# The last block of the second and third feed-forward also prepares the next attention's first batch

## The chip, the cores and the metric

One core of a Trainium2 chip runs the whole program. The metric is the device time of one execution in microseconds, lower is better. The program is one launch that computes four layers, each an attention and a feed-forward network, on 8 batches of 256 tokens of 128 numbers, with 512 context tokens a batch.

## The reference, cut to what matters

All eight steps add to `x`, and each one normalises `x` over its last axis first:

```python
x = x + _L0_xattn_ref(_layernorm(x), ctx, ctx, ...)     # A0
x = x + _L0_ffn_ref(_layernorm(x), ...)                 # F0, quantised
x = x + _L1_xattn_ref(_layernorm(x), ctx, ...)          # A1
x = x + _L1_ffn_ref(_layernorm(x), ...)                 # F1, 8 experts + shared one
x = x + _L2_xattn_ref(_layernorm(x), ctx, ctx, ..., mask)  # A2
x = x + _L2_ffn_ref(_layernorm(x), ...)                 # AS (causal attention) and F2, 8 experts
x = x + _L3_xattn_ref(ctx, ctx, _layernorm(x), mask, ...)  # A3
x = x + _L3_ffn_ref(_layernorm(x), ...)                 # F3, 8 experts
```

An attention has 16 heads of 8 numbers. Its queries come from `x`, its keys and values from the context (in AS all three come from `x`):

```python
scores = jnp.einsum('bhqd,bhkd->bhqk', q, k) / scale    # plus a mask in A2 and A3
attn = jax.nn.softmax(scores, axis=-1)
ctx = jnp.einsum('bhqk,bhkd->bhqd', attn, v)
```

An expert layer computes gates for each token and adds up `comb[t, e] * (act(x @ w1[e] + b1[e]) @ w2[e] + b2[e])` over its experts.

## The kernel before

The kernel is written in nine phases (`PHASES`): A0, F0, A1, F1, A2, AS, F2, A3, F3. Each engine has its own instruction stream, written out in order by hand, and the streams meet at semaphores. For each phase and each kind of event the class `Counts` knows which count a semaphore has by then, so `wait(pe, "max_done", cnt.at(...) - BACK[i])` means: PE goes on when the maximum that last read this buffer is done.

**An attention phase** goes through 8 batches, and each batch through 4 groups of 4 heads. For each group PE makes *plain* scores (queries as rows, `scores`, L1036, 8 matmuls into the three PSUM banks `ps_s`), DVE takes the maximum of each row (`maximum`, L1435, or L1438 with A2's mask added), POOL splits the maxima into bf16 parts (`split_maxima`, L685 to L688), PE turns them (`maxima_T`, L1086 and L1088, into the bank `ps_m`), ACT copies them into `qmx` (L890), and only then PE makes the *transposed* scores with the maximum already taken off (`scores_T`, L1051, banks `ps_t`; in A2 a mask is put in first, `opening_mask`, L1062). ACT takes their exponential (L845), and PE multiplies with the values (`values`, L1078, bank `ps_av`). In the steady state the plain scores run two groups ahead.

Before a batch can start it needs its keys, queries and values. `misc` makes them on PE in `ps_m`: "K" (L1120, fp32, 128x512), "XT" (L1108, two transposes of the normalised tokens), "Q" (L1113, 128x256) and "V" (L1126, four of 128x128). ACT reads each of them out (L868, L859, L863, L875). POOL normalises the tokens (L700) and splits keys and queries into a high and a low part (`split_k`, L666 and L668; `split_q`, L674 and L676). The SP queue saves these to DRAM (`save`, L488) and loads them back as strips of heads (`load_strips`, L523 and L524, into `kst` and `qst`). `output_bias` (L1094, L1097; DVE L1423) makes a constant that is added to the result. `take_misc` makes PE wait for the last reader of `ps_m`.

**An expert phase** (F1, F2, F3) goes through 4 blocks of 512 tokens, and each block through its experts (9 in F1, 8 in F2 and F3). `first_product` (L1281) makes the hidden layer of expert `e + 1` in `ps_t` and `ps_s[2]` while ACT applies the activation to that of expert `e` (L985, or L983 in F2); `second_product` (L1303) multiplies it by the second weights into `ps_s[0]` or `ps_s[1]`, and DVE adds it up with its gate (`accumulate`, L1667 and L1669). After the last expert `result` adds to `x_tok` (L1691) and takes the statistics of the tokens (L1367 to L1379), and POOL makes the reciprocal deviation (`power`, L640). The split weights (`w_parts`, L970 and L785) lie in `kst[1]`, and the third pair of F1 in `kst[0]`; the split tokens `x_hi`, `x_lo` are `k_hi`, `k_lo`; `combT` is part of `kf`. Every one of these is also an attention's buffer.

Between an expert phase and the next attention all engines wait for the last block's result, although batch 0 needs only the tokens of block 0:

```python
            def attention(ph):
                if ph != "AS":
                    wait(pe, "acc_done", cnt.start("acc_done", ph))
                    wait(pe, "h_done", cnt.start("h_done", ph))
                    wait(pe, "x_new", cnt.start("x_new", ph))
```

After that come K, XT, Q, V, the biases, then 16 plain scores of groups 0 and 1 with `maxima_T` of group 0 after the thirteenth, and then the batches. POOL waits likewise before it normalises batch 0 (`rstd_done`), and DVE before its first maximum.

## Time and profile before

| | |
|---|---|
| runs | 1944.78, 1940.82, 1942.22 us, median 1942.22 |
| profiled execution | 1943.53 us, of which the span is 1941.7 us |
| PE busy | 1749.6 us (90%) |
| DVE, ACT, POOL busy | 1149.1 (59%), 1084.7 (56%), 589.3 us (30%) |
| F1's last matmul, A2's first exponential | 834.1, 863.1 us |
| F2's last matmul, A3's first exponential | 1455.7, 1487.7 us |

The times of a row count from the start of the span. PE is busy nearly all the time, so the places of interest are those where it is not: among them are the two stretches in the last rows of the table, 29 and 32 us, in which one phase has ended and the next has not got going. The chip grants TensorE one of two clocks, 1.2 or 2.4 GHz; "PEclk" is the mean of it as a share of 2.4 GHz.

### The profile page before, as it was taken

The numbers are of one execution on the slowest core, as the hardware profiler recorded it, in microseconds if no ns is written. First come the engines' busy times: TensorE is split into PE (matmuls) and PEld (weight loads), VectorE is DVE, ScalarE is ACT, GpSimd is POOL, SyncE is SP. The second block draws the span as 40 slices with busy tenths as digits, with TensorE's granted clock in tenths as the row PEclk, the third lists the DMA queues.
The fourth block names the chain that finished last, engine by engine and source line by source line (L and its number), as shares of the span: only waits on it lengthen the run. The fifth ranks groups of instructions, "written<-read, shape, count | busy, mean of one in ns | idle before, by whom it ended". The sixth has DMA issues, their size and how long they took to land.

```text
span 1941.7 us, 38864 instructions
## 1 busy us (share of the span) xinstructions
PE 1749.6 (90%) x14438; PEld 1188.5 (61%) x14476; DVE 1149.1 (59%) x3394; ACT 1084.7 (56%) x2172; POOL 589.3 (30%) x1171
## 2 busy tenths in 40 slices
PE   5999955899979999979999999979996999989997
PEld 2555524455548889944444455558883555569997
DVE  5788846688852332236777656636664888633443
ACT  1788831488864444426677755533332888844442
POOL 5344212233312221122333344323324344122221
PEclk9999977699999999969999999979995999989999
DMA  4443200455300000023323134300004454100000
GB/s 142 128 126 121 76 16 14 128 169 175 104 18 1 1 1 1 1 87 113 102 92 99 40 115 134 92 1 1 1 1 129 146 155 137 35 1 7 6 7 6
DMA packets 114854, 132.38 MB, mean 68 GB/s; under 512 B 14934, under 2 KB 78700, under 8 KB 114668
## 3 DMA queue, kind: packets, MB, share of 16 engines
q1 hardware_dynamic: 114668, 129.90, 22.1%
q8 instruction: 117, 1.92, 0.4%
q14 instruction: 69, 0.57, 0.1%
HBM read 83.45 MB, written 46.40 MB: 67 GB/s over the span
## 4 chain that ended last, share of the span: by engine, by line
PE 76%; issue 7%; DVE 7%; ACT 6%; POOL 1%; DMA 1%; SPq 0%; POOLq 0%; DVEq 0%
PE ps_s L1303 14%; PE ps_av L1078 13%; PE ps_s L1036 12%; PE ps_t L1281 9%; PE ps_t L1051 4%; PE ps_s L1281 3%; ACT prob L845 3%; PE ps_t L1062 3%; DVE mx L1435 3%; PE ps_m L1086 2%; PE ps_m L1134 2%; PE ps_m L1120 2%; PE ps_m L1126 2%; PE ps_m L1113 2%; PE ps_t L1064 1%
## 5 line engine op out<-in xcount | busy, mean ns | idle before, releaser
L845 ACT ACTIVATE prob<-ps_t 128x512 f32<-128x512 f32 (+1 forms) x1152 | 616.5, 586 | 169.8 <-PE ps_t L1051 161.7
L1435 DVE TENSOR_REDUCE mx<-ps_s 128x1 f32<-128x512 f32 x768 | 487.3, 683 | 110.9 <-PE ps_s L1036 109.4
L1036 PE MATMUL ps_s<-kst,qst 32*128 32x512 f32 (+2 forms) x1280 | 387.1, 490 | 43.3 <-DVE mx L1435 22.4
L1303 PEld LDWEIGHTS ps_s<-w_ffn,prob 128*128 128x128 f32 x2688 | 314.2, 192 | 8.3
L1303 PE MATMUL ps_s<-w_ffn,prob 128*128 128x128 f32 x2688 | 318.4, 276 | 0.0
L1036 PEld LDWEIGHTS ps_s<-kst,qst 32*128 32x128 f32 x1280 | 166.7, 192 | 241.4 <-issue 98.1
L1051 PE MATMUL ps_t<-qmx,kst 32*128 32x256 f32 (+1 forms) x2304 | 306.4, 334 | 6.1 <-ACT prob L845 6.1
L1078 PE MATMUL ps_av<-prob,vaug 128*32 128x256 f32 (+1 forms) x4608 | 307.2, 386 | 2.7 <-ACT avs L886 2.7
L985 ACT ACTIVATE prob<-ps_t,b1c 128x512 f32<-128x512 f32 x204 | 125.3, 685 | 240.9 <-PE ps_t L1281 240.9
L1669 DVE SCALAR_TENSOR_TENSOR avs<-ps_s,comb,avs 128x128 f32<-128x128 f32 x336 | 94.6, 344 | 260.4 <-PE ps_s L1303 260.4
L785 POOL TENSOR_TENSOR kst<-w_ffn,kst 128x512 fp32r<-128x512 f32 x100 | 127.1, 1273 | 371.3 <-ACT kst L970 371.3
L1438 DVE CUSTOM_DVE_ANT_0 junk<-ps_s,mask_q 128x512 bf16<-128x512 f32 x256 | 167.6, 687 | 67.6 <-PE ps_s L1036 66.0
L1051 PEld LDWEIGHTS ps_t<-qmx,kst 32*128 32x128 f32 x2304 | 188.5, 189 | 15.4 <-ACT prob L845 10.1
L685 POOL CAST mpart<-mx 128x8 bf16<-128x8 f32 x160 | 34.8, 217 | 517.3 <-DVE mx L1435 304.8
L1281 PE MATMUL ps_t<-k_hi,kst 128*128 128x512 f32 x600 | 184.8, 416 | 6.2 <-ACT xfT L947 2.4
L1078 PEld LDWEIGHTS ps_av<-prob,vaug 128*32 128x32 f32 x4608 | 122.3, 111 | 93.8 <-ACT avs L886 5.1
L1281 PEld LDWEIGHTS ps_t<-k_hi,kst 128*128 128x128 f32 x600 | 107.8, 193 | 27.6 <-DVE prob L1654 3.6
L1438 DVE CUSTOM_DVE_ANT_0 junk<-ps_s,caus_q 128x128 bf16<-128x128 f32 (+1 forms) x256 | 82.3, 354 | 70.9 <-PE ps_s L1036 69.1
L640 POOL TENSOR_TENSOR rstd<-veps,neg_half 128x2 f32<-128x2 f32 (+1 forms) x60 | 48.4, 807 | 246.2 <-DVE means L1379 246.2
L890 ACT ACTIVATE qmx<-ps_m 128x256 fp32r<-128x256 f32 x160 | 61.5, 385 | 109.5 <-PE ps_m L1088 109.3
L1062 PE MATMUL ps_t<-mask_T,ident_b 128*128 128x512 bf16 x218 | 76.8, 394 | 14.4 <-ACT prob L845 12.0
L1281 PE MATMUL ps_t<-k_lo,kst 128*128 128x512 f32 x300 | 86.1, 396 | 0.0
(209 smaller groups left out, 2151.3 us busy)
## 6 DMA issues: line engine op xcount, KB each, us to landing
kst<-k_parts SPq DMA_DIRECT2D x128, 256.0 KB, 3.4
qst<-q_parts SPq DMA_DIRECT2D x160, 128.0 KB, 3.6
k_parts<-k_hi SPq DMA_DIRECT2D x64, 256.0 KB, 3.0
q_parts<-q_hi SPq DMA_DIRECT2D x80, 128.0 KB, 2.4
ctxT<-in_ctxT SPq DMA_DIRECT2D x32, 256.0 KB, 2.7
k_parts<-k_lo SPq DMA_DIRECT2D x32, 256.0 KB, 3.5
q_parts<-q_lo SPq DMA_DIRECT2D x40, 128.0 KB, 2.4
w_ffn<-in_F_w SPq DMA_DIRECT2D x18, 256.0 KB, 3.3
```

Of the source, the lines that this page charges most:

```text
L785: pool.tensor_tensor(halves(wl), first_weights(ph, e), halves(wh.bitcast(F32)), ALU.subtract).then_inc(sig["wl_done"], 1)
L845: nc.scalar.activation(row[:, S * kt:S * kt + w], ps_t[TURN[unit(ph, g, n) % 8]][:, 0:w], ACT.Exp).then_inc(sig["exp_done"], 1)
L985: nc.scalar.activation(h[:, c, :], src, ACT.Gelu, bias=b1c[:, 4 * e + c:4 * e + c + 1]).then_inc(sig["h_done"], 1)
L1036: pe.matmul(dst, qst[p][strip, g, q * 128:(q + 1) * 128], kst[p][strip, g, 0:nk], start=True, stop=True).then_inc(sig["s_ready"], 1)
L1051: mm = pe.matmul(dst, kst[p][strip, g, kt * 128:(kt + 1) * 128], qmx[strip, g % 2, seen(ph, kt):], start=not opened, stop=not opened or c ...
L1062: pe.matmul(bank[:, :].rearrange("p (c s) -> p c s", c=2), ident_b[:, :], mask_T[:, 2 * kp:2 * kp + 2, :], start=True, stop=False)
L1078: mm = pe.matmul(ps_av[32 * j:32 * j + 32, q0:S], vaug[p][:, kt, HG * g + j, :], prob[:, buf, j, S * kt:S * (kt + 1) - q0], start=(kt == 0 ...
L1281: mm = pe.matmul(ps_h[c][:, :], w[:, 128 * c:128 * (c + 1)], x[:, :], start=(n == 0), stop=(n == 2))
L1303: mm = pe.matmul(dst, h[:, c, 128 * q:128 * (q + 1)], w2c, start=(c == 0 and not bias), stop=(c == nc_h - 1))
L1435: dve.tensor_reduce(mx[:, buf, i:i + 1], src, AX.X, ALU.max, negate=True).then_inc(sig["max_done"], 1)
L1438: dve.tensor_tensor_reduce(junk[:, TURN[i], 0:nk], src, m, -1.0, 3.0e38, ALU.add, ALU.min, mx[:, buf, i:i + 1])\
L1669: ins = dve.scalar_tensor_tensor(out=acc[:, q, :], in0=src, scalar=comb[:, q, n:n + 1], in1=acc[:, q, :], op0=ALU.mult, op1=ALU.add)
```

## The change

The last block of F1 and F2 also makes K, XT, Q and V of the next attention's batch 0, each behind one expert's second product, and its output bias (in F1 also that of AS) around the fifth expert. POOL normalises batch 0 at the start of that block and splits keys and queries between the experts' weights; ACT reads the four results out between the experts. For this the buffers that both phases used are separate now (`x_hi`, `x_lo`, `w_third`, `combT`). The 16 plain scores of groups 0 and 1 are issued right behind the block (`LED_PAIRS = 0`: none within it), and no longer go through `ps_s` but by turns through `ps_av` and `ps_m`, so that a score waits for the maximum two before it. `maxima_T` of group 0 comes behind all 16. DVE takes the 16 maxima behind the block's result and statistics. A1 is unchanged (F0 has no such block), and so is AS.

```diff
+LEADS = {
+    "F1": {(0, "end"): "K", (1, "end"): "XT", (2, "end"): "Q", (3, "end"): "V", (4, "mid"): "B0", (4, "end"): "B1"},
+    "F2": {(0, "end"): "K", (1, "end"): "XT", (2, "end"): "Q", (3, "end"): "V", (4, "mid"): "B0"},
+}
+LED = {"A2": "F1", "A3": "F2"}
+LED_PAIRS = 0
...
-        x_hi, x_lo = k_hi, k_lo
-        w_parts = [(kst[p][:, n, :], kst[p][:, n + 1, :]) for p, n in ((1, 0), (1, 2), (0, 0))]
+        x_hi = sb("x_hi", [128, SK], F32R)
+        x_lo = sb("x_lo", [128, SK], F32R)
+        w_third = sb("w_third", [128, 2, SK], F32R)
+        w_parts = [(kst[1][:, 0, :], kst[1][:, 1, :]), (kst[1][:, 2, :], kst[1][:, 3, :]), (w_third[:, 0, :], w_third[:, 1, :])]
...
@@ POOL: attention
+                if ph in LED:
+                    split_maxima(ph, b0, 0)
+                    normalise_batch(ph, b1)
                     if ph == "A3":
-                        prepare_masks(b0)
+                        prepare_masks(b1)
+                    split_maxima(ph, b0, 1)
@@ POOL: experts
+                def lead(at):
+                    ph_next = {"F1": "A2", "F2": "A3"}[ph]
+                    if at == "XT":
+                        if ph_next == "A3":
+                            prepare_masks(Batch(0))
+                        normalise_batch(ph_next, Batch(0))
+                    elif at == "K":
+                        split_k(ph_next, Batch(0))
+                    elif at == "Q":
+                        split_q(ph_next, Batch(0))
...
+                    if last and ph in LEADS:
+                        lead("XT")
                     for e in range(turn, ne if last else ne + turn):
                         low_weights(blk + e // ne, e % ne)
+                        if last and ph in LEADS:
+                            lead({turn + 1: "K", turn + 3: "Q"}.get(e))
@@ ACT: experts, behind expert e
+                        if last and ph in LEADS and e:
+                            lead(e - 1)
@@ PE: scores (DVE's maximum reads the same bank)
-                wait(pe, "max_done", cnt.at("max_done", ph, bt, 8 * g + i) - BACK[i])
-                dst = ps_s[TURN[i]][:, 0:nk]
+                if led(ph, bt, g):
+                    bank = (ps_av, ps_m)[i % 2]
+                    wait(pe, "max_done", cnt.at("max_done", ph, bt, 8 * g + i) - 2)
+                    if i % 2:
+                        take_misc("max_done", cnt.at("max_done", ph, bt, 8 * g + i))
+                else:
+                    bank = ps_s[TURN[i]]
+                    wait(pe, "max_done", cnt.at("max_done", ph, bt, 8 * g + i) - BACK[i])
+                dst = bank[:, 0:nk]
@@ PE: attention
+                if ph in LED:
+                    for pair in range(LED_PAIRS, 8):
+                        lead(ph, pair)
+                    wait(pe, "acc_done", cnt.start("acc_done", ph))
+                    wait(pe, "h_done", cnt.start("h_done", ph))
+                    wait(pe, "g_done", cnt.start("g_done", ph))
+                    maxima_T(ph, b0, 0)
@@ PE: experts (DVE likewise, around accumulate)
+                        if last and ph in LEADS:
+                            lead({"F1": "A2", "F2": "A3"}[ph], LEADS[ph].get((e, "mid")))
...
                         second_product(blk, e, e)
+                        if last and ph in LEADS:
+                            lead({"F1": "A2", "F2": "A3"}[ph], LEADS[ph].get((e, "end")))
```

Three places show how the instructions move. The first is PE between F1 and A2, from the last second product (`prob`) to A2's first transposed scores. Before:

```order
L1120 MATMUL ps_m<-ctxT,w_A 128x512
L1108 MATMUL ps_m<-ident,xn 128x128 x2
L1113 MATMUL ps_m<-xnT,w_A 128x256
L1126 MATMUL ps_m<-w_A,ctxT 128x128 x4
L1094 MATMUL ps_m<-bo_A,ones_row 128x128
L1097 MATMUL ps_m<-w_A,bv_wide 128x128
L1094 MATMUL ps_m<-bo_AS,ones_row 128x128
L1036 MATMUL ps_s<-kst,qst 128x512 x13
L1086 MATMUL ps_m<-qst,ident_r 128x256
L1088 MATMUL ps_m<-ident_b,mpart 128x128 x2
L1036 MATMUL ps_s<-kst,qst 128x512 x3
L1062 MATMUL ps_t<-mask_T,ident_b 128x512 x2
```

The same place now, with the waits and the number of each buffer; between the first two rows and the third stand twelve more scores, by turns into `ps_av` and `ps_m`, each with its wait for `max_done`:

```order
L1381 MATMUL ps_s0<-w_ffn,prob 128x128 x4
L1090 MATMUL ps_av<-kst0,qst0 128x512 [waits stacked0_0,max_done,ct_read,lg_read]
L1090 MATMUL ps_m<-kst0,qst0 128x512 [waits bias_ready,max_done]
L1090 MATMUL ps_av<-kst0,qst0 128x512 [waits max_done]
L1090 MATMUL ps_m<-kst0,qst0 128x512 [waits max_done]
...
L1140 MATMUL ps_m<-qst0,ident_r 128x256 [waits max_done,g_done,msplit,h_done,acc_done]
L1142 MATMUL ps_m<-ident_b,mpart 128x128 x2
L1116 MATMUL ps_t0<-mask_T,ident_b 128x512 [waits exp_done]
```

The seven rows of K to the biases are gone from here, and the maxima's turn, which stood before the last three scores, now waits for all 16 maxima, since the last of them reads `ps_m`.

The second place is where those seven rows went, PE in F1's last block, here around experts 0 to 2:

```order
L1381 MATMUL ps_s<-w_ffn,prob 128x128 x16
L1174 MATMUL ps_m<-ctxT,w_A 128x512
L1359 MATMUL ps_t<-x_hi,w_third 128x512 x3
...
L1381 MATMUL ps_s<-w_ffn,prob 128x128 x16
L1162 MATMUL ps_m<-ident,xn 128x128 x2
L1359 MATMUL ps_t<-x_hi,kst 128x512 x3
...
L1381 MATMUL ps_s<-w_ffn,prob 128x128 x16
L1167 MATMUL ps_m<-xnT,w_A 128x256
```

Each stands between one expert's second product and the first product after the next.

The third is POOL in F2's last block and behind it: the block's last six weights (`kst<-w_ffn,kst`), the deviation (`rstd`) and A3's start. Before:

```order
L640 TENSOR_TENSOR rstd<-veps,neg_half 128x4
L785 TENSOR_TENSOR kst<-w_ffn,kst 128x512 x6
L640 TENSOR_TENSOR rstd<-veps,neg_half 128x4
L653 TENSOR_SCALAR mrow<-mrow_i 16x512
L700 TENSOR_SCALAR xn<-x_tok,means,rstd 128x128 x2
L666 CAST k_hi<-kf 128x512
L668 TENSOR_TENSOR k_lo<-kf,k_hi 128x512
```

Now:

```order
L652 TENSOR_TENSOR rstd<-veps,neg_half 128x4
L665 TENSOR_SCALAR mrow<-mrow_i 16x512
L714 TENSOR_SCALAR xn<-x_tok,means,rstd 128x128 x2
L801 TENSOR_TENSOR kst<-w_ffn,kst 128x512 x2
L678 CAST k_hi<-kf 128x512
L680 TENSOR_TENSOR k_lo<-kf,k_hi 128x512
L801 TENSOR_TENSOR kst<-w_ffn,kst 128x512 x2
```

The mask's and the tokens' rows now stand ahead of the low weights of experts 2 and 3, and the keys' split between those of 3 and 4.

## Rows read from the trace of the kernel before

**Rows 1.** The page: PE's share of the span, and PEclk in 40 slices

```profile
PE 1749.6 (90%) x14438; PEld 1188.5 (61%) x14476; DVE 1149.1 (59%) x3394; ACT 1084.7 (56%) x2172; POOL 589.3 (30%) x1171
...
PEclk9999977699999999969999999979995999989999
```

**Rows 2.** Chain of waits from F1 to A2: start us, us, what

```profile
838.31 1.59 POOL xn L700 x2
...
847.55 2.65 DMA qst<-q_parts
...
855.56 0.14 issue
855.70 0.78 PE ps_s L1036
...
856.60 0.69 DVE junk L1438
...
858.76 0.51 PE ps_m L1086
859.27 0.24 PE ps_m L1088 x2
...
866.52 0.85 PE ps_t L1062 x2
```

**Rows 3.** Timeline of PE, F1's last block to A2: start us, us, engine, line, operation

```profile
779.72 3.73 PE L1303 MATMUL ps_s<-w_ffn,prob 128*128 128x128 f32 x32
783.21 0.93 PE L1281 MATMUL ps_t<-k_hi,kst 128*128 128x512 f32 x3
...
861.73 1.31 PE L1036 MATMUL ps_s<-kst,qst 32*128 32x512 f32 x2 [0.17 <-DVE mx L1438]
```

**Rows 4.** Timeline of DVE and of ACT from F1 to A2

```profile
836.96 0.16 DVE L1379 COPY means<-mv 128x4 f32<-128x4 f32 x1
...
851.18 0.69 DVE L1438 CUSTOM_DVE_ANT_0 junk<-ps_s,mask_q 128x512 bf16<-128x512 f32 x1 [2.14 <-PE ps_s L1036]
...
863.12 0.60 ACT L845 ACTIVATE prob<-ps_t 128x512 f32<-128x512 f32 x1 [1.89 <-PE ps_t L1051]
```

**Rows 5.** Timeline of DVE and of ACT from F2 to A3

```profile
1459.76 0.16 DVE L1379 COPY means<-mv 128x4 f32<-128x4 f32 x1
...
1475.91 4.87 DVE L1435 TENSOR_REDUCE mx<-ps_s 128x1 f32<-128x512 f32 x8 [4.00 <-PE ps_s L1036]
...
1484.13 0.38 ACT L890 ACTIVATE qmx<-ps_m 128x256 fp32r<-128x256 f32 x1 [13.58 <-PE ps_m L1088]
1484.53 1.28 ACT L845 ACT_TABLE_LOAD   x1
1487.69 0.60 ACT L845 ACTIVATE prob<-ps_t 128x512 f32<-128x512 f32 x1 [1.88 <-PE ps_t L1051]
```

**Rows 6.** Chain of waits from F2 to A3

```profile
1486.28 1.15 PE ps_s L1036 x2
```

**Rows 7.** Timeline of PE in F2's last two blocks

```profile
1405.76 0.60 PE L1233 MATMUL ps_m<-ident,avs 128*128 128x128 f32 x4
1406.11 0.95 PE L1281 MATMUL ps_t<-k_hi,kst 128*128 128x512 f32 x3
```

**Rows 8.** Timeline of POOL in F2's last block and behind it

```profile
1422.49 1.28 POOL L785 TENSOR_TENSOR kst<-w_ffn,kst 128x512 fp32r<-128x512 f32 x1
...
1461.10 1.93 POOL L653 TENSOR_SCALAR mrow<-mrow_i 16x512 f32<-16x512 int32 x1
```

**Rows 9.** Stretches: busy us (instructions) by engine, then PEclk, DMA share, GB/s

```profile
863.12:878.00 14.88, 13.12 (x44) 5.44 (x45) 6.07 (x20) 7.07 (x14) 4.76 (x10) 0.50 0.44 130
878.00:885.00 7.00, 6.31 (x66) 2.94 (x66) 3.93 (x12) 4.91 (x11) 2.52 (x5) 0.99 0.69 232
...
1264.00:1276.00 12.00, 11.67 (x74) 6.45 (x74) 4.72 (x31) 3.44 (x9) 1.53 (x5) 0.50 0.00 0
...
1487.69:1503.00 15.31, 13.78 (x64) 6.47 (x66) 7.20 (x12) 8.99 (x18) 7.20 (x13) 0.51 0.51 156
```

More of the change, by code:

```diff
@@ L344, in unit, with led @@
             return HG * pairs(ph) * g + n
+        def led(ph, bt, g):
+            return ph in LED and bt.b == 0 and g < 2
         def unit_at(ph, k, half):
@@ L1148, in misc, with lead @@
                     mm.then_inc(sig["o_ready"], 1)
-            def attention(ph):
-                if ph != "AS":
+            def lead(ph, what):
+                b0 = Batch(0)
+                if what == "K":
+                    misc_reader[0] = None
+                    if ph == "A2":
+                        for a in watt_in:
+                            pe.wait_ge(watt_in[a], 64)
+                    if ph == "A3":
+                        pe.wait_ge(bd_loaded, 16 * 3 * H)
+                if what in ("K", "XT", "Q", "V"):
+                    misc(what, ph, b0)
+                elif what in ("B0", "B1"):
+                    output_bias(ph if what == "B0" else "AS")
+                elif what is not None:
+                    if what == 0:
+                        wait(pe, "lg_read", cnt.start("lg_read", ph))
+                        wait(pe, "ct_read", cnt.start("ct_read", ph))
+                    for i in (2 * what, 2 * what + 1):
+                        scores(ph, b0, i // 8, i % 8)
+            def attention(ph):
+                b0 = Batch(0)
+                if ph in LED:
+                    for pair in range(LED_PAIRS, 8):
[3 more added lines that the diff above has]
+                    wait(pe, "g_done", cnt.start("g_done", ph))
+                    maxima_T(ph, b0, 0)
+                elif ph != "AS":
                     wait(pe, "acc_done", cnt.start("acc_done", ph))
@@ L1169, in attention @@
                     mm.then_inc(w1_across, 1)
-                for g in range(0 if ph == "AS" else 2):
+                for g in range(0 if ph == "AS" or ph in LED else 2):
                     for i in range(8):
@@ L1490, in convert_rest, with lead @@
                 link(dve.tensor_scalar(mask_T[:, :, :], mask_T_i, 0.0, MASKED, ALU.is_equal, ALU.mult))
+            def lead(ph, what):
+                if what in ("B0", "B1"):
+                    output_bias(ph if what == "B0" else "AS")
+                elif isinstance(what, int):
+                    for i in (2 * what, 2 * what + 1):
+                        maximum(ph, Batch(0), i // 8, i % 8)
             def attention(ph):
                 b0 = Batch(0)
-                if ph != "AS":
+                if ph in LED:
+                    for pair in range(LED_PAIRS, 8):
+                        lead(ph, pair)
+                elif ph != "AS":
                     wait(dve, "x_new", cnt.start("x_new", ph))
@@ L1498, in attention @@
                     quantise_weights()
-                for a in {"A2": ("A2", "AS"), "AS": ()}.get(ph, (ph,)):
-                    output_bias(a)
-                for g in range(0 if ph == "AS" else 2):
-                    for i in range(8):
-                        maximum(ph, b0, g, i)
+                if ph != "AS" and ph not in LED:
+                    output_bias(ph)
+                    for g in range(2):
+                        for i in range(8):
+                            maximum(ph, b0, g, i)
                 def body(bt, first, last):
@@ L1705, in body @@
                             dve.tensor_copy(combT[:, :], ps_av[0:E + 1, :]).then_inc(sig["ct_read"], 1)
+                        if last and ph in LEADS:
+                            lead({"F1": "A2", "F2": "A3"}[ph], LEADS[ph].get((e, "mid")))
                         accumulate(blk, e)
+                        if last and ph in LEADS:
+                            lead({"F1": "A2", "F2": "A3"}[ph], LEADS[ph].get((e, "end")))
                         if not last and e == 3:
```

41 lines of the change are left out of this document (22 added, 19 removed).

## The prediction

> **What bounds the kernel now.** I read the page first: PE is busy for 90% of the span, so time is lost where it is not, and where the digits of PEclk fall from 9 to 5, 6 or 7 [rows 1]. Two of these places lie at the seams that the change touches. The chain of waits across the first seam is a string of single steps on different engines: POOL normalises tokens in 1.59 us, at the end a 2.65 us transfer brings the strips, and only then the first score runs [rows 2]. The timelines give the length. F1's tokens and statistics are complete at 836.96 + 0.16 = 837.12, the first maximum starts at 851.18, and the first exponential at 863.12 [rows 4]. At F2 the same three are 1459.92, 1475.91 and 1487.69 [rows 5]. So there are 14.1 and 16.0 us of preparation, and then 11.9 and 11.8 us from the first maximum to the first exponential. The clock is low in both seams and for 15 us more, 0.50 to 878 and 0.51 to 1503, the lower of its two levels (1.2 GHz); then it is up again [rows 9]. DVE, not PE, sets the pace of the 16 maxima before: 8 take 4.87 us, 0.61 each, from three banks [rows 5].
>
> I take the first exponential of the next attention as the mark, because the order of everything from there on is as before, and so a shift of the mark is a shift of the end, as long as the clock behaves alike.
>
> **Longer last blocks.** PE is the bottleneck of an expert block, so each moved matmul costs its full warm time there. A second product of 16 fp32 matmuls of 128 columns starts at 779.72 and the next product at 783.21: 3.49 us, or 0.218 each [rows 3]. By columns K is four of these, Q two, V four, the first bias two in A2 (one in A3), that of AS one: 13 in F1 and 11 in F2. Two transposes cost half of the 0.35 us of four [rows 7], 0.18. F1 gets 13 x 0.218 + 0.18 = 3.0 us, F2 11 x 0.218 + 0.18 = 2.6 us.
>
> Waits inside the blocks I cost at nearly nothing. ACT has its readings of K, XT, Q and V between one expert's activations and the next, and PE needs `ps_m` again only a whole expert later, several us. In F2 POOL is the tight one: the low weights of expert 2 started at 1422.49 and now stand behind the mask's 1.93 [rows 8] and the tokens' 1.59 us [rows 2], so they end at 1422.49 + 3.52 + 1.28 = 1427.3, about when PE, with K ahead of it, wants them. I put 0.1 us; the bounds are 0 and 1.9 (the mask's whole time). DMA: the saves and strips, whose last transfer takes 2.65 us [rows 2], now start three or more experts before the block ends, so neither the SP queue nor a transfer shows. If that cover failed, the first score would wait for the rest of it.
>
> **16 maxima from two banks.** The first two scores run behind the last second product while DVE still does the statistics, so the first maximum starts 0.03 us after them: at 837.12 + 3.0 + 0.03 = 840.15 in A2 and 1459.92 + 2.7 + 0.03 = 1462.65 in A3. Then each bank goes round: a maximum ends, PE starts its next score 0.14 later, it takes 0.78, DVE starts at 856.60, which is 1.04 after the 855.56 at which the maximum ended, and takes 0.69 [rows 2]: 1.73 us for two maxima where three banks gave two in 1.22. Seven rounds and the last pair are 7 x 1.73 + 0.61 + 0.69 = 13.4 us. The bounds of a round are 1.22 (DVE's own pace, seven rounds 3.6 us shorter) and 1.73 plus half.
>
> This depends on the clock, and row and skill can be weighed. The 0.78 was measured at the low clock. At the upper level a score could take no less than half, a round 1.34, and the sum would be 2.7 us better at each seam. I take the low clock: PE has no work for some 2 us before the first round and then two short scores in each.
> The Trainium skill ("TensorE: Matmul & The Clock Gate", section "A second HAM failure mode: psum-queue depth-cycling") speaks against this change here: cycling through banks leaves small idle gaps between groups of matmuls in which the clock may fall and have to be regained. By that rule the rounds are slow ones, as in my sum; the trace agrees as far as it shows this (0.50 through the scores before), but it has no two-bank stretch.
>
> **From the last maximum to the exponential.** In A2: 0.14, then the turned maxima 0.51 + 0.24, two masks 0.85 [rows 2], then from the start of the two next scores to the exponential 863.12 - 861.73 = 1.39 [rows 3, 4]: 3.1 us. In A3 there is no mask: 0.14 + 0.75 + 1.41 (1486.28 to 1487.69) = 2.3 [rows 5, 6], but ACT has to copy (0.38) and load its table (1.28) [rows 5], 0.14 + 0.75 + 0.04 + 0.38 + 1.28 + 0.05 = 2.6, which is now late instead. Before, the table and the turning lay beside the last scores; now nothing covers them.
>
> **The sum.** A2's first exponential: 840.15 + 13.4 + 3.1 = 856.7, 6.4 us earlier. A3's: 1462.65 + 13.4 + 2.6 = 1478.7, 9.0 us earlier. Together 15.4 us. The profiled execution took 1943.5 us, so 1928.1; it stands 1.3 us above the median, against which I forecast 1942.2 - 15.4 = **1926.8 us**, 0.8% faster. Of the 30 us of preparation about half is given back, 5.7 us as work in the blocks and the rest because scores and turning are slower or uncovered. A measurement of this kernel can tell some 0.2%, or 4 us, from no change.
>
> **Rivals.**
> 1. *The clock is regained sooner.* If it stays up or comes back within the rounds, a seam gains 2.7 us and up to half of the 15 us behind the first exponential. PE is busy 13.1 of 14.9 us there, but ACT alone needs 7.1 [rows 9], so I count 5: 7.7 us a seam, 1919 for one seam and 1911 for both. For it speaks that PE starts dense work with no gap; against it that PE's 13.1 busy us did not bring it back any sooner before. Chance 0.08.
> 2. *The clock returns at the same moment as before* (878.0 and 1503.0, [rows 9]) and not at the same distance from the exponential. Then 6.4 and 9.0 more us run at the low clock, about half of it lost, 7.7 us: 1934.5. Chance 0.08.
> 3. *PE waits in the blocks* because POOL or ACT is late: the mask's 1.9 us in F2, and some 1 us for one hand-over of `ps_m` in each: 1931. Chance 0.06.
> 4. *Slower: the clock stays down long behind the seam.* Cold running costs half its time, so the gain of 15.4 is gone when the two low stretches are together 31 us longer. From 1264 to 1276 the clock was at 0.50 though PE was busy for 11.67 of 12 us [rows 9], so dense work is no guarantee. With 20 us more at each seam the price is 20 us: 1947. Against it: both seams now regain it about 15 us behind the exponential. Chance 0.04.
>
> **Numbers.** The forecast has 0.74. Its own range, from the bounds of the round (1.22 to warm) and of the waits, and from a clock that changes a few us off, is 1920 to 1933. To leave out no more than 2 in 10 I go from 1918 (half of rival 1) to 1935 (rivals 2 and 3). Faster by over 0.2% means under 1938.3: all but rival 4 and a remainder of mishaps, 0.93; within 0.2% 0.03; slower 0.04.
>
> **What would show it.** In the changed profile: F1's last block 3.0 us longer and F2's 2.7; no idle PE inside them beyond 0.3 us; the first maximum at 840.2 and 1462.7, right at the end of the statistics; pairs of maxima every 1.73 us, 13.4 us for all; the exponentials at 856.7 and 1478.7; the table load right ahead of A3's first exponential; clock back some 15 us later. It is wrong if the pairs come much faster or slower, if low weights in F2's last block keep PE waiting, or if the low clock lasts on beyond 875 and 1497.

## The result, and the profile after

| | median us | range us | executions |
|---|---|---|---|
| before | 1943.75 | 1939.98 to 1959.77 | 16 |
| after | 1934.04 | 1929.32 to 1943.84 | 16 |

The ratio is 0.9941, 95% interval 0.9916 to 0.9965: faster by 0.6% where 0.8% was forecast, 1934.0 us where 1926.8 was, inside the stated range of 1918 to 1935 by one microsecond. The profiled execution of after took 1931.52 us, its span 1929.7; that of before 1943.53 and 1941.7. So the two traces differ by 12.0 us, and that is what the next table accounts for. (Two executions of kernels below, of experiments 9 and 10, took several ms and are left out.)

```profile
PE 1759.5 (91%) x14476; PEld 1185.7 (61%) x14476; DVE 1149.9 (60%) x3394; ACT 1084.6 (56%) x2172; POOL 589.5 (31%) x1171
...
PEclk9999977699998999979999999979996999989999
```

These two lines of after's page answer to [rows 1]. PE is busy 10 us longer in a span that is 12 us shorter. PEclk has a 7 in its 18th place, the first seam, where it had a 6, and a 6 in its 31st, the second, where it had a 5.

Now from mark to mark. "Result" is the start of DVE's last addition to `x_tok` in a block.

| from, to | before | after | difference | forecast |
|---|---|---|---|---|
| start to the result of F1's block 3 | 773.71 | 774.58 | +0.87 | 0 |
| F1's last block | 61.12 | 65.28 | +4.16 | +3.0 |
| its result to A2's first exponential | 28.29 | 17.78 | -10.51 | -9.4 |
| from there to the result of F2's first block | 478.14 | 475.58 | -2.56 | 0 |
| F2's second and third block | 77.89 | 80.23 | +2.34 | 0 |
| F2's last block | 38.48 | 43.45 | +4.97 | +2.7 |
| its result to A3's first exponential | 30.06 | 17.69 | -12.37 | -11.7 |
| from there to the result of F3's first block | 289.81 | 289.74 | -0.07 | 0 |
| F3's other three blocks and the end | 164.20 | 165.37 | +1.17 | 0 |
| sum | | | -12.00 | -15.4 |

Both seams gave more than forecast, by 1.8 us together. The blocks took back 7.8 us more than forecast, and not only the last ones. (Between the traces the forecast was missed by 3.4 us. The median is 7.2 us over the forecast: the traced execution of after lies 2.5 us under its median, and the forecast counts from a median 1.3 us under the traced execution of before.)

**The first seam.** DVE's timeline in after (the changed kernel), to be held against [rows 4]:

```profile
839.86 0.69 DVE L1781 TENSOR_TENSOR x_tok<-x_tok,avs 128x512 f32<-128x512 f32 x1
...
842.06 0.68 DVE L1518 CUSTOM_DVE_ANT_0 junk<-ps_av,mask_q 128x512 bf16<-128x512 f32 x1
...
843.63 0.69 DVE L1518 CUSTOM_DVE_ANT_0 junk<-ps_av,mask_q 128x512 bf16<-128x512 f32 x1 [0.27 <-PE ps_av L1090]
...
854.17 0.69 DVE L1518 CUSTOM_DVE_ANT_0 junk<-ps_m,mask_q 128x512 bf16<-128x512 f32 x1 [0.18 <-PE ps_m L1090]
```

The first maximum starts at 842.06, right at the end of the statistics, as forecast. The preparation that took 14.1 us is gone. The last maximum starts at 854.17, so 16 of them take 12.8 us, and a round of two takes 1.64 (842.67 to 854.17 over seven), where 1.73 was forecast. PE and ACT in the same place, for [rows 2, 3]:

```profile
839.03 0.49 PE L1090 MATMUL ps_av<-kst,qst 32*128 32x512 f32 x1
...
842.80 0.79 PE L1090 MATMUL ps_av<-kst,qst 32*128 32x512 f32 x1 [3.28 <-DVE mx L1518]
...
855.12 0.55 PE L1140 MATMUL ps_m<-qst,ident_r 128*128 128x256 f32 x1 [0.99 <-DVE mx L1518]
...
856.70 0.79 PE L1105 MATMUL ps_t<-qmx,kst 32*128 32x256 f32 x4
...
856.35 1.28 ACT L876 ACT_TABLE_LOAD   x1
857.64 0.60 ACT L876 ACTIVATE prob<-ps_t 128x512 f32<-128x512 f32 x1
```

PE waits 3.28 us for the first maximum, and its scores take 0.79 us each from then on, at the low clock, where the first took 0.49 at the upper one. The clock falls at 840.6, within this wait and before the rounds begin. At the end the turned scores start at 856.70 and could be read 0.8 us later. The exponential starts at 857.64, though, when ACT has its table: the load is the last thing in A2 too, by 0.14 us. The sum had named it for A3 alone.

**The second seam**, DVE and ACT of after against [rows 5]:

```profile
1459.09 0.68 DVE L1515 TENSOR_REDUCE mx<-ps_av 128x1 f32<-128x512 f32 x1
...
1471.12 0.69 DVE L1515 TENSOR_REDUCE mx<-ps_m 128x1 f32<-128x512 f32 x1 [0.20 <-PE ps_m L1090]
...
1473.30 1.28 ACT L876 ACT_TABLE_LOAD   x1
1474.59 0.60 ACT L876 ACTIVATE prob<-ps_t 128x512 f32<-128x512 f32 x1
```

The same picture: 12.72 us for the maxima, 2.78 from their end to the exponential, the table load right ahead of it.

**The clock** behind the seams in after, columns as in [rows 9]:

```profile
857.64:865.00 7.36, 6.58 (x23) 2.55 (x23) 2.62 (x8) 3.71 (x7) 2.45 (x4) 0.53 0.34 107
865.00:878.00 13.00, 11.14 (x96) 4.99 (x96) 9.17 (x28) 9.11 (x18) 5.85 (x14) 1.00 0.67 213
1474.59:1490.00 15.41, 13.83 (x67) 6.24 (x65) 7.08 (x12) 9.45 (x19) 7.55 (x12) 0.53 0.56 166
1490.00:1503.00 13.00, 12.25 (x129) 7.14 (x129) 10.27 (x17) 10.85 (x23) 4.06 (x11) 1.00 0.34 106
```

At A2 it is up again at 865, 7 us behind the exponential, where it took 15 before. At A3 it took until 1490, 15 us, as before. Of the -2.56 us in the table 1.5 lie in A2 and AS and 1.0 in F2's first block (F2's first product starts 434.0 us behind the exponential where it was 435.5). But this is not shown to come from the change. The traces of experiments 1 and 2 below have the same place:

```profile
859.75:877.00 17.25, 15.49 (x62) 6.46 (x67) 7.61 (x23) 9.03 (x17) 6.27 (x11) 0.50 0.51 158
```

```profile
864.73:872.00 7.27, 6.49 (x22) 2.57 (x22) 2.13 (x8) 3.71 (x7) 2.53 (x5) 0.52 0.35 112
```

The first is another execution of the changed kernel: there the clock is low for 17 us behind the exponential. The second is the kernel before with nothing but separate buffers, its seam as it was: there it is low for 7 us. From the exponential to the result of F2's first block these two took 480.85 and 474.97 us, where the table has 478.14 before and 475.58 after. So the difference of 8 us in the clock's return is one that executions show without the change.

**The blocks.** PE's timeline in F1's last block, where each second product (`prob`) starts and what follows it:

```profile
780.63 3.73 PE L1381 MATMUL ps_s<-w_ffn,prob 128*128 128x128 f32 x32
784.20 1.02 PE L1174 MATMUL ps_m<-ctxT,w_A 128*128 128x512 f32 x2
...
787.82 3.73 PE L1381 MATMUL ps_s<-w_ffn,prob 128*128 128x128 f32 x32
791.39 0.38 PE L1162 MATMUL ps_m<-ident,xn 128*128 128x128 f32 x2
...
794.41 3.73 PE L1381 MATMUL ps_s<-w_ffn,prob 128*128 128x128 f32 x32
...
801.22 3.73 PE L1381 MATMUL ps_s<-w_ffn,prob 128*128 128x128 f32 x32
804.79 1.06 PE L1180 MATMUL ps_m<-w_A,ctxT 128*128 128x128 f32 x8
...
808.52 0.48 PE L1148 MATMUL ps_m<-bo_A,ones_row 1*128 1x128 f32 x2
808.94 0.49 PE L1151 MATMUL ps_m<-w_A,bv_wide 128*128 128x128 f32 x2
809.26 3.74 PE L1381 MATMUL ps_s<-w_ffn,prob 128*128 128x128 f32 x32
812.93 0.48 PE L1148 MATMUL ps_m<-bo_AS,ones_row 1*128 1x128 f32 x2
813.34 0.97 PE L1359 MATMUL ps_t<-x_hi,kst 128*128 128x512 f32 x3
```

From product to product an expert takes 7.19 us with K (780.63 to 787.82), 6.59 with XT, 6.81 with Q, and 8.04 with V and the first bias; without anything it takes some 6.34 (the mean of two). So K, XT and Q cost 0.85, 0.25 and 0.47, as forecast (0.87, 0.18, 0.44). V and the bias cost 1.70 and not 1.31. The two biases are what is dearer: from a one-row matmul to the next instruction it is 0.41 to 0.42 us (808.52 to 808.94, 812.93 to 813.34) where the sum had 0.22 by its columns. The expert with the bias of AS took 7.42 us (809.26 to 816.68) where it took 6.74 before: 0.68 more, again some 0.4 over the columns.

In F2 POOL was the tight engine. The timelines of POOL and, in the last two lines, PE in after, against [rows 8]:

```profile
1416.91 1.94 POOL L665 TENSOR_SCALAR mrow<-mrow_i 16x512 f32<-16x512 int32 x1
1418.95 1.64 POOL L714 TENSOR_SCALAR xn<-x_tok,means,rstd 128x128 f32<-128x128 f32 x2
1420.56 2.51 POOL L801 TENSOR_TENSOR kst<-w_ffn,kst 128x512 fp32r<-128x512 f32 x2
...
1416.38 0.50 PE L1359 MATMUL ps_t<-x_hi,kst 128*128 128x512 f32 x1 [0.71 <-DVE prob L1744]
...
1424.31 0.86 PE L1359 MATMUL ps_t<-x_hi,kst 128*128 128x512 f32 x3
```

The mask and the tokens go ahead of two low weights, which end at 1421.8 and 1423.07. PE started the product behind K at 1422.98 and its second part, which reads the first of them, at 1424.31, with no idle time shown. So nothing waited there, and the bound of 1.9 us was not used. The prediction's 1427.3 for their end counts from the kernel before; this block starts 5.7 us earlier in after, which makes it 1421.6, and 1421.8 was measured. The 0.71 us that PE waits at 1416.38 is for the gates at a block's start. In this trace it is followed by 3.4 us of low clock. The third and the last block of F2 have one such dip each, which costs some 1.5 us (the second took 39.34 us, the third 40.89). The wait is not the whole reason: the second block has the same 0.71 us (at 1336.15) and no dip, and the kernel before waits 0.77 us (at 1422.08) and has none.

### The profile page after: what moved, and what is told of

Read it like the earlier page. It is cut to its first block, busy times and chain, and to the rows that moved or that the text cites. A ratio compares the mean times of both kernels' runs of the same rounds, so it can differ in the third digit from the quotient of the medians.

```text
span 1929.7 us, 38917 instructions
## 1 busy us (share of the span) xinstructions
PE 1759.5 (91%) x14476; PEld 1185.7 (61%) x14476; DVE 1149.9 (60%) x3394; ACT 1084.6 (56%) x2172; POOL 589.5 (31%) x1171
## 4 chain that ended last, share of the span: by engine, by line
PE 80%; DVE 7%; ACT 5%; issue 5%; POOL 1%; DMA 0%; SPq 0%; POOLq 0%; DVEq 0%
PE ps_s L1381 15%; PE ps_av L1132 13%; PE ps_s L1090 12%; PE ps_t L1359 10%; PE ps_t L1105 4%; PE ps_s L1359 4%; PE ps_t L1116 3%; DVE mx L1515 3%; ACT prob L876 2%; PE ps_m L1140 2%; PE ps_m L1188 2%; PE ps_m L1174 2%; PE ps_m L1180 2%; PE ps_m L1167 1%; PE ps_t L1118 1%
## 5 line engine op out<-in xcount | busy, mean ns | idle before, releaser
L1515 DVE TENSOR_REDUCE mx<-ps_s 128x1 f32<-128x512 f32 x752 | 477.4, 683 | 107.2 <-PE ps_s L1090 105.7
L1090 PE MATMUL ps_s<-kst,qst 32*128 32x512 f32 (+2 forms) x1248 | 369.6, 481 | 32.1 <-DVE mx L1515 19.2
L1090 PEld LDWEIGHTS ps_s<-kst,qst 32*128 32x128 f32 x1248 | 158.7, 188 | 222.1 <-issue 93.8
L801 POOL TENSOR_TENSOR kst<-w_ffn,kst 128x512 fp32r<-128x512 f32 x88 | 111.9, 1274 | 311.4 <-ACT kst L1006 311.4
L1518 DVE CUSTOM_DVE_ANT_0 junk<-ps_s,mask_q 128x512 bf16<-128x512 f32 x240 | 157.6, 687 | 63.5 <-PE ps_s L1090 60.6
L1359 PE MATMUL ps_t<-x_hi,kst 128*128 128x512 f32 x528 | 166.2, 422 | 6.0 <-ACT xfT L983 2.3
L1359 PEld LDWEIGHTS ps_t<-x_hi,kst 128*128 128x128 f32 x528 | 95.6, 194 | 27.5 <-DVE prob L1744 3.4
L1116 PE MATMUL ps_t<-mask_T,ident_b 128*128 128x512 bf16 x256 | 87.1, 389 | 9.1 <-ACT prob L876 7.9
L1028 ACT ACTIVATE prob<-ps_t 128x512 f32<-128x512 f32 x64 | 34.7, 595 | 83.7 <-PE ps_t L1359 83.4
```

Of the source, the lines that this page charges most:

```text
L801: pool.tensor_tensor(halves(wl), first_weights(ph, e), halves(wh.bitcast(F32)), ALU.subtract).then_inc(sig["wl_done"], 1)
L1090: pe.matmul(dst, qst[p][strip, g, q * 128:(q + 1) * 128], kst[p][strip, g, 0:nk], start=True, stop=True).then_inc(sig["s_ready"], 1)
L1116: pe.matmul(bank[:, :].rearrange("p (c s) -> p c s", c=2), ident_b[:, :], mask_T[:, 2 * kp:2 * kp + 2, :], start=True, stop=False)
L1359: mm = pe.matmul(ps_h[c][:, :], w[:, 128 * c:128 * (c + 1)], x[:, :], start=(n == 0), stop=(n == 2))
L1515: dve.tensor_reduce(mx[:, buf, i:i + 1], src, AX.X, ALU.max, negate=True).then_inc(sig["max_done"], 1)
L1518: dve.tensor_tensor_reduce(junk[:, TURN[i], 0:nk], src, m, -1.0, 3.0e38, ALU.add, ALU.min, mx[:, buf, i:i + 1])\
```

## The experiments

Each ran beside the kernel before, on the same chip (median 1946.15 us in the first batch, 1945.81 in the second, 1945.16 in the third).

**1. The changed kernel once more**, as a control.

> The changed kernel once more, as the control of this group. Theory A (the gain is the two seams' shorter way to the first exponential, less the longer blocks): about 10 us below the kernel before. Its runs so far spread over 14 us, from 1929 to 1944, those of the kernel before over 6. Theory A says that the slow ones are those in which the low clock lasts longer, so the mean granted clock falls with the time: some 0.949 at 1929 us, 0.941 at 1941 us. The rival (something else varies, a wait in the blocks) expects no such relation.

1934.42 us (1929.82 to 1940.51, 6 executions), ratio 0.9933 (0.9913 to 0.9953): the result stands. The granted clock goes with the time as theory A says, 0.949 at 1929.8 us and 0.942 at 1940.4, with one execution beside it (0.947 at 1937.1). The profiled execution took 1940.51. Of the 9 us over that of after, 2.4 lie before F1's last block, 3.8 in A2 and AS and 3.1 in F2: 1.5 in its first block and 1.6 because the second has a dip of the clock, too (40.91 us).

**2. The buffers alone.** The kernel before, with the buffers apart and nothing moved.

```diff
-        x_hi, x_lo = k_hi, k_lo
+        x_hi = sb("x_hi", [128, SK], F32R)
+        x_lo = sb("x_lo", [128, SK], F32R)
+        w_third = sb("w_third", [128, 2, SK], F32R)
...
-            combT = kf[0:E + 1, :]
+            combT = sb("combT", [E + 1, SK])
```

> The kernel before with the change's separate buffers and nothing else. In the changed kernel's trace every expert block is 0.32 to 0.41 us longer, also those that the change doesn't touch. Theory B: this comes from where the new buffers lie, so this kernel is 11 x 0.37 = 4 us slower than before, and its F1, F2 and F3 blocks last 61.9, 39.3 and 54.5 us where they lasted 61.5, 38.9 and 54.1. The rival (it comes from the moved work or from the clock) expects the blocks and the time of the kernel before, within 1 us.

Ratio 1.0049 (1.0027 to 1.007): slower by 0.5% without any work moved. The blocks are those of the changed kernel: 61.87 us in F1, 39.35 and 39.33 in F2, 54.50 in F3, against 61.55, 38.95 and 54.13 before. Twelve blocks and 0.37 us each are 4.4 us. The twelve executions lie at 1945 to 1948, 1956 to 1959 and 1967 to 1968, so the median, 1957.0, holds more than the blocks: the granted clock is 0.940 to 0.944 in the first group, 0.935 or 0.936 in the second and 0.927 to 0.929 in the third. The profile is of the first group. Why this kernel falls into the others in eight of twelve executions stays open.

**3. The places changed over.** In the changed kernel, `x_hi` and `x_lo` stand where `k_hi` and `k_lo` stood before, and these at the new places.

```diff
-        k_hi = sb("k_hi", [128, SK], F32R)
-        k_lo = sb("k_lo", [128, SK], F32R)
+        x_hi = sb("x_hi", [128, SK], F32R)
+        x_lo = sb("x_lo", [128, SK], F32R)
...
-        x_hi = sb("x_hi", [128, SK], F32R)
-        x_lo = sb("x_lo", [128, SK], F32R)
+        k_hi = sb("k_hi", [128, SK], F32R)
+        k_lo = sb("k_lo", [128, SK], F32R)
```

> The changed kernel, with x_hi and x_lo at the addresses that k_hi and k_lo had, and these two at the new ones. If the place of the tokens is the cause, the blocks are back at 61.5, 38.9 and 54.1 us and the kernel gains about 4 us on the control. If it is that of the third weights or of the gates' buffer, the blocks stay long and the time is the control's.

1930.93 us (1923.19 to 1941.38), ratio 0.9922. F3's blocks are back at 54.12 and 54.11 us, and F1's at 61.68 (0.13 over the kernel before; `w_third` and `combT` still have places of their own, and no run separates them). F2's second and third took 40.56 and 40.55 us, each with a dip of the clock; in experiments 8 and 11, with the same places and no dip, they took 38.95 to 39.00. PE's timeline of after in F3, and then that of this kernel:

```profile
1766.88 0.94 PE L1359 MATMUL ps_t<-x_hi,kst 128*128 128x512 f32 x3
...
1767.89 0.86 PE L1359 MATMUL ps_t<-x_hi,kst 128*128 128x512 f32 x3
...
1768.83 0.86 PE L1359 MATMUL ps_t<-x_lo,kst 128*128 128x512 f32 x3
...
1769.76 0.49 PE L1381 MATMUL ps_s<-w_ffn,prob 128*128 128x128 f32 x3
```

```profile
1767.49 0.94 PE L1359 MATMUL ps_t<-x_hi,kst 128*128 128x512 f32 x3
...
1768.49 0.84 PE L1359 MATMUL ps_t<-x_hi,kst 128*128 128x512 f32 x3
...
1769.40 0.84 PE L1359 MATMUL ps_t<-x_lo,kst 128*128 128x512 f32 x3
```

From product to product after needs 1.01, 0.94 and 0.93 us, this kernel 1.00 and 0.91. The instructions are the same, and so are the buffers' sizes. Only the address of the moving operand differs, and with it 1 to 3% of the time of each product of 4 matmuls. So the extra time in the blocks is shown to come from the places; why one place is slower than another stays open. The median moved by 3.5 us, where the blocks give 3.9 (4.4 less 0.13 in each of F1's four), but the two intervals overlap, so it is the blocks that show this and not the median.

**4. Three banks for the early scores**: the bank of F1's hidden layer, `ps_s[2]`, is free behind the block, too.

```diff
-                    bank = (ps_av, ps_m)[i % 2]
-                    wait(pe, "max_done", cnt.at("max_done", ph, bt, 8 * g + i) - 2)
+                    bank = (ps_av, ps_m, ps_s[2])[(8 * g + i) % 3]
+                    wait(pe, "max_done", cnt.at("max_done", ph, bt, 8 * g + i) - 3)
```

> The plain scores behind the blocks by turns in three banks (ps_av, ps_m, ps_s[2]) rather than two. Theory A: the round over two banks (1.64 us a pair, measured) is a cost of the change at both seams. With three, DVE's own pace of 0.61 us returns, the 16 maxima take 9.8 us instead of 12.8, and the turning of the maxima can start two maxima sooner: each seam 4 us shorter, together about 8 us faster than the control. The rival (the time behind the seam depends on when the clock comes back, not on the first exponential) expects under 2 us.

1925.33 us (1921.76 to 1942.47), ratio 0.9885 (0.9866 to 0.9903), 9.1 us under the control. The timelines of DVE and (last line) ACT of this kernel in the first seam:

```profile
840.04 0.69 DVE L1781 TENSOR_TENSOR x_tok<-x_tok,avs 128x512 f32<-128x512 f32 x1
...
842.24 0.68 DVE L1518 CUSTOM_DVE_ANT_0 junk<-ps_av,mask_q 128x512 bf16<-128x512 f32 x1
...
842.85 0.68 DVE L1518 CUSTOM_DVE_ANT_0 junk<-ps_m,mask_q 128x512 bf16<-128x512 f32 x1
...
852.01 0.08 DVE L1518 DVE_READ_ACCUMULATOR2_ANT mx<- 128x1 f32 x1
...
853.65 0.60 ACT L876 ACTIVATE prob<-ps_t 128x512 f32<-128x512 f32 x1
```

DVE now goes without a gap, 0.61 us a maximum, 1.22 a pair. The exponential comes 13.6 us behind the block's result where it was 17.8 (13.4 against 17.7 at A3). So the two banks did cost what the round's sum says, 4.2 us a seam. This very execution took 1942.47 us, though, and these stretches say why:

```profile
1150.00:1156.00 6.00, 5.18 (x61) 3.04 (x61) 3.46 (x24) 3.17 (x8) 2.84 (x9) 1.00 0.52 145
1156.00:1201.00 45.00, 44.55 (x255) 25.66 (x255) 18.17 (x104) 16.61 (x41) 11.86 (x34) 0.51 0.33 97
```

The clock is low for 45 us in the middle of AS, with PE busy for 44.55 of them. Two of its six executions lay at 1942 (granted clock 0.936) and four at 1922 to 1928 (0.945 to 0.949).

**5. PE kept busy through the seam.** Twelve matmuls into `ps_t[0]`, whose result nobody reads, behind the first two early scores, and one behind each later one.

```diff
                     for i in (2 * what, 2 * what + 1):
                         scores(ph, b0, i // 8, i % 8)
+                        if what:
+                            filler(1)
+                    if what == 0:
+                        filler(12)
```

> The changed kernel with matmuls that nobody reads, into ps_t[0]: 12 behind the first two scores, where PE waits 3.3 us for the end of the statistics, and one behind each later score. Each is 0.23 us at the upper clock. Theory C: the idle 3.3 us and the thin rounds behind it are what lets the clock fall, and with PE kept busy it stays up through both seams. Then a pair of maxima takes some 1.35 us rather than 1.64, the low stretches of 24 to 31 us at the seams are gone, and the kernel is 5 to 7 us faster at each seam, 10 to 15 us together. The rival (the clock falls whatever PE does there, or the filler stands in the way of the scores) expects no gain, or 1 to 3 us more.

1942.53 us (1938.56 to 1963.27), ratio 1.0008: all of the gain is lost. Two stretches of its first seam:

```profile
843.00:850.00 7.00, 6.72 (x21) 3.46 (x19) 6.29 (x24) 0.00 (x0) 1.03 (x1) 1.00 0.00 0
850.00:867.00 17.00, 16.74 (x31) 6.53 (x30) 7.72 (x24) 2.26 (x3) 3.30 (x10) 0.50 0.00 1
```

The filler did hold the clock up, to 850, and until then the scores took 0.49 us and a pair of maxima 1.70. But then it fell with no gap in PE's work: 16.74 of 17 us are busy at 0.50. From there on score and filler take 1.45 us together, and the exponential came 5 us later than in after. At A3 it fell at 1478, and the exponential came 6.6 us later behind the result. So giving PE something to do did not keep the clock up through the seams, and the filler stood in the way of the scores. This profile is of one of the four longest executions (1954 to 1963 us, granted clock 0.933 to 0.939). The other eight lie at 1939 to 1945 with 0.946 to 0.950, no lower than the 0.941 to 0.949 of the changed kernel, and take longer than it all the same; the filler itself is some 12 us by estimate, 26 matmuls of 0.23 us in each of two seams.

**6. The early scores within the block**, 12 of 16 in F1's last block and 8 in F2's, the rest behind the turning of group 0.

```diff
-LED_PAIRS = 0
+LED_PAIRS = {"A2": 6, "A3": 4}
...
-(4, "end"): "B1"},
+(4, "end"): "B1",
+           (5, "end"): 0, (6, "mid"): 1, (6, "end"): 2, (7, "mid"): 3, (7, "end"): 4, (8, "mid"): 5},
```

> The changed kernel with most of the plain scores within the last block: 12 of 16 from behind expert 5 of F1 on, 8 of 16 in F2, in the same two banks; POOL splits the maxima of group 0 before it waits for the block's statistics, and PE turns them right behind the block, ahead of the scores that are left. DVE has some 5 us free in each expert of F1 and 1.7 to 2.5 in F2. Theory A: the maxima behind the block are what is left of the seam. In F1 12 scores add some 12 x 0.25 = 3 us to the block and take 6 rounds of 1.64, 9.8 us, from behind it; the exponential moves up by 7 us in A2 and some 4 in A3, 11 together. The rival (PE waits within the block for maxima that stand behind accumulate on DVE, over 0.5 us a pair) expects under 4 us.

1926.79 us (1922.56 to 1936.91), ratio 0.9906 (0.9884 to 0.9927). The exponentials come at 854.70 and 1468.46, 2.9 and 6.1 us earlier than in after (3 of the latter from the first seam), less than the expected 7 and 4. The reason is in the blocks: F1's last is 8.2 us longer than in after and F2's 5.2, where the scores themselves are 3 and 2 us. In F1 PE waits 1.6 us within the block for maxima, as the rival said, and from 841 on it works at the low clock: a quarter of the last second product takes 2.08 us, where it took 1.16. Its median is 7.6 us under the control's, though the intervals just overlap, and it does not beat the third bank.

**7. The first seam alone**: the entries of F2 and A3 taken out of `LEADS` and `LED`, the buffers left apart.

> The change at F1 and A2 alone; F2 and A3 as before, but with the separate buffers. Theory A: the first seam is worth 5.5 us to the first exponential and some 3 us for a clock that is back sooner, less the buffers' 4 us (all 12 expert blocks); so about 4 to 5 us under the kernel before, and the second seam's 9 us and its sooner clock are missing against the control. The rival (one seam carries the gain) expects this kernel either level with before or level with the whole change.

1946.08 us (1941.39 to 1950.34, 12 executions), ratio 1.0001 (0.999 to 1.0011): no gain, where theory A expected 4 to 5 us. In its profile the first seam is that of after (table load at 856.39) and the second that of before (26.8 us from result to table load). The profiled execution is the lowest of the twelve, 2.1 us under that of before. The seam's 10.5 us and 3.0 from the clock behind it stand there against 3.8 for the longer block, 4.4 for the places and 3.1 for two dips in F2, though F2 has no moved work here. So the level median does not say that the first seam gains nothing: the places and the dips use it up.

**8. Scores in the block and the places changed over**, 6 and 3 together.

> in_block with the tokens' halves at the old addresses. If the two are independent, it is faster than in_block by the 0.38 us of each block of F3 and 0.2 to 0.35 of the others, 3 to 4 us, and some 15 us faster than the control. If they are not, it is level with in_block.

1916.98 us (1916.65 to 1925.97, 5 executions), ratio 0.9871 (0.9851 to 0.9891): the lowest median of all (the interval overlaps those of experiments 4 and 11), 0.9% under the control. F2's blocks are 38.95 and 38.96 again, with no dip of the clock at their boundaries, which is a part of why it gained 9.8 us on in_block and not 3 to 4, and the exponentials come at 854.53 and 1461.19.

**9. The bias's one-row matmul five times.**

```diff
+                if ph in ("A2", "AS", "A3"):
+                    for _ in range(4):
+                        pe.matmul(ps_m[:, 0:D], ones_row[:, 0:128], bo_att[ph][:, :], start=True, stop=True)
```

> The changed kernel, with each one-row matmul of an output bias (that of A2 and of AS in F1's last block, that of A3 in F2's) issued five times, the last time as before. Theory D: such a matmul costs 0.42 us in the stream, as the rows of the changed kernel say (808.52 to 808.94), not the 0.218 us of a full one that my sum took by its columns. Then F1's last block goes from 65.3 to 65.3 + 8 x 0.42 = 68.7 us and F2's from 43.5 to 45.2, the median 5.0 us over that of the changed kernel. Rival: the interval in the rows is a cost of the switch between two kinds of operands and not of the matmul; then repeats cost 0.22 or less each, F1's last block is 67.0 or less and the median at most 2.6 us up.

1933.85 us as the median of five (1932.84 to 1940.83), ratio 0.9957 (0.9941 to 0.9974). The median is that of the changed kernel and the ratio is 0.0024 over the control's, with intervals that overlap, so the blocks have to decide. PE's timeline in F1's last block:

```profile
808.59 1.15 PE L1150 MATMUL ps_m<-bo_A,ones_row 1*128 1x128 f32 x8
809.58 0.38 PE L1151 MATMUL ps_m<-bo_A,ones_row 1*128 1x128 f32 x2
809.89 0.49 PE L1154 MATMUL ps_m<-w_A,bv_wide 128*128 128x128 f32 x2
...
813.89 1.15 PE L1150 MATMUL ps_m<-bo_AS,ones_row 1*128 1x128 f32 x8
814.88 0.38 PE L1151 MATMUL ps_m<-bo_AS,ones_row 1*128 1x128 f32 x2
```

Four more take 0.99 us, 0.25 each, and the block grew by 1.80 us for eight, 0.23 each (F2's by 0.89 for four). My theory of 0.42 us for such a matmul falls: repeats cost what the sum said, and some 0.2 us is paid once, however many follow. The rival puts this to the change from one kind of operands to another. The second product ahead of the bias fits, with 3.67 us from its start to the next (809.26 to 812.93) where it had 3.49 in [rows 3], but no run separates the change of operands from other reasons.

**10. The first seam alone with the places changed over.**

> The change at F1 and A2 alone, with x_hi and x_lo at the places that k_hi and k_lo had before, and these at the new ones. Theory B: the first seam alone was level with the kernel before (ratio 1.0001) because its gain of some 6.7 us is eaten by the new places of the buffers; here the blocks of F2 and F3 should be back at 38.9 and 54.1 us and the median 4 us under the kernel before, ratio 0.998. Rival: the first seam's gain is lost behind it, in the clock of A2 and AS, whatever the places; then the ratio stays at 1.000 although the blocks are short again.

Ratio 0.9999 (0.9978 to 1.002). A median says little here: six executions lie at 1936.9 to 1940.2 and five at 1950.7 to 1953.4, on average 6.5 us under the kernel before (1938.6 against 1945.16) and 6.6 over it. The lower group is even below what theory B gave. The granted clock is 0.940 to 0.943 in the lower group and 0.931 to 0.934 in the upper. By an estimate from these that is some 35 us more at half the clock, enough for the 13 us; where they lie the profile, which is of a lower one, does not show. In it F3's blocks are back at 54.11 us, and F2's second and third took 40.56 and 40.57, with a dip each. So the ratio goes with the rival, the lower group with theory B, and the experiment does not decide.

**11. Three banks and the places changed over**, 4 and 3 together.

> The changed kernel with the early scores by turns in three banks and x_hi, x_lo at the old places of k_hi, k_lo. If the gains add up: 9.1 us for the banks (measured) and 3.5 us for the places (measured) under the changed kernel's 1934.4, so 1922, with first exponentials 12.3 + 1.3 us behind the block's result. Rival: the low clock moves to other places (44 us in AS, as in one execution of the three-bank kernel) and takes half of it back: 1928 or more.

1920.58 us (1919.48 to 1925.29, 4 executions), ratio 0.9882 (0.9867 to 0.9897), near the 1922 that was added up. The ratio is that of three banks alone (0.9885), so the places' share shows in F3's blocks (54.11 and 54.12 us) and not in it. The exponentials stand 13.6 and 13.4 us behind the results, and here no execution lay at 1940.

## Why the prediction was right, and what it missed

- **The range**: the terms gave 1920 to 1933, and 1934.04 lies outside that. The 1935 stood there for rivals 2 and 3, and the trace of after shows neither. So the mechanism at the seams was right, and that the number is still inside is in part luck.
- **The preparation goes from the seams**: right. The first maximum comes right at the end of the statistics in both, and the seams are 10.5 and 12.4 us shorter (forecast 9.4 and 11.7).
- **"Longer last blocks", 3.0 and 2.6 us by columns**: undersized. Without the effect of the places they are 3.8 (4.16 - 0.33) and 3.1 us longer (4.97, less 0.4 for the places and 1.5 for the dip of the clock). K, XT and Q cost what the rows before said; what was missed is some 0.4 us in each of F1's two experts with a bias and 0.3 in F2's one; of this 0.2 is paid once beside the one-row matmul (experiment 9).
- **Waits in the blocks, 0.1 us**: right, no idle PE in after that before had not. Rival 3 is out.
- **The round, 1.73 us a pair**: 1.64 measured, 12.8 us for 16 maxima where 13.4 was forecast. The sum added the whole 0.69 us of a maximum to the 1.04 from its end to the next in the same bank. The first round took 1.57 (842.06 to 843.63), the seven on average 1.64. That the scores would run at the low clock (0.79 us) was right. That the second bank was the limit, experiment 4 shows: 1.22 a pair with three, and 4.2 us a seam.
- **The last maximum to the exponential, 3.1 and 2.6 us**: 2.78 in both. In A2, too, the table load is last.
- **The term that the sum did not have**: the buffers that are now apart. The prediction gave them no line at all, and they cost 0.3 to 0.4 us in each of twelve expert blocks, 4.4 us, which experiment 2 shows by itself. Next come the two dips of the clock in F2 (3.0 us) and the 1.2 us of the leads' size. Against them stand 1.8 us more from the seams and 3.0 from the clock behind A2: -15.4 + 4.4 + 3.0 + 1.2 - 1.8 - 3.0 is -11.6, where the trace has -12.0. The two terms of the clock cancel, and both differ between executions whose code is the same there, so neither is shown to be an effect of the change.
- **"The order of everything from there on is as before, and so a shift of the mark is a shift of the end, as long as the clock behaves alike"**: the condition did not hold. In the trace of after the clock came back 8 us sooner behind A2's exponential (3.0 us less up to the result of F2's first block, when its 0.4 for the places is taken off), at A3 as forecast. That looks like a part of rival 1, but experiment 2 has it without the change, and experiment 1 has not: there the clock was back at A2 at 877, almost the 878.0 of rival 2. In after itself it came back 13 us earlier than at 878.0 and 1503.0 in both, so rival 2 is out for this trace, and not for every execution. Rival 4's 1947 us was reached by none of the 22 executions of the changed kernel (at most 1943.84), but in experiments 4 and 5 such long low stretches did occur, in AS.

The Trainium skill ("TensorE: Matmul & The Clock Gate", section "A second HAM failure mode: psum-queue depth-cycling") was cited for slow rounds, and the trace agrees, with 0.79 us a score. But the clock had fallen before the first round, at 840.6 in PE's wait of 3.28 us, so the fall does not show its rule of small gaps. The filler closed these gaps and the clock fell nevertheless, at 850, and in AS in experiment 4 it stayed at 0.51 for 45 us with PE busy for 44.55. What makes it fall in dense work no run here shows.

## What to carry to other kernels

When a change takes apart buffers that were shared, put its address effect into the sum and measure it alone, by a kernel that has the new buffers and nothing else. Here it took 4.4 of the 16.4 us that the trace would have gained without it, about a quarter. When a chain of waits is emptied, ask what goes round behind it: two banks held DVE at 0.82 us a maximum, a third gave 4.2 us a seam, 9.1 us in the median, nearly what the change itself had brought. Cost moved matmuls by the time between starts in the trace, with something on top for one of another kind that stands alone, and not by their columns alone. And before a few microseconds of clock are put down to a change, look at the same place in a second execution.

## What was not expected of the hardware

- The address of a matmul's moving operand changes its pace: products of 4 matmuls 0.93 or 0.91 us (after, experiment 3), blocks 54.50 or 54.12.
- A wait of 0.71 to 0.78 us at a block's start stands in F2 in every trace looked at here. In some it was followed by 3.4 us of low clock, in others not (before, experiments 2, 5, 8 and 11), and in after in two blocks of three.
- How long the clock stays low behind A2's exponential differs by 10 us between two executions of the changed kernel (7 in after, 17 in experiment 1).
- Executions of one kernel group around values 10 to 20 us apart (1922 and 1942 in experiment 4, 1938 and 1951 in experiment 10, 1945, 1957 and 1967 in experiment 2), the upper ones with a lower granted clock, so a median of six can fall on either.
